# Local attention blocks: turned probabilities placed by DMAs, and half of the rotated keys' sum on VectorE

## What is computed

```
def attn_layer(x, Wqkv, qs, ksc, Wo):
    q, k, v = jnp.split(x @ Wqkv, 3, -1)         # then split into heads
    q = l2norm(q) * qs
    k = l2norm(k) * ksc
    q = q * cos * scale + rotate_half(q) * sin * scale
    k = k * cos * inv + rotate_half(k) * sin * inv
    out = local_attention(q, k, v)
    return out @ Wo
# local_attention: queries of window w against keys of windows w-1 and w
    sim = jnp.einsum('bhwie,bhwje->bhwij', bq, bk2) * QK_SCALE
    attn = jax.nn.softmax(jnp.where(mask, -max, sim), -1)
    out = jnp.einsum('bhwij,bhwje->bhwie', attn, bv2)
for i in range(6):
    x = attn_layer(shift_tokens(x), ...) + x
    x = ffn_layer(shift_tokens(x), ...) + x
```

## Time and profile before

| | us |
|---|---|
| median of 3 runs | 3162.67 |
| lowest, highest run | 3152.88, 3163.48 |
| the profiled execution, own time | 3146.83 |
| its span | 3144.8 |
| local blocks in it | 861 to 2760 |
| PE busy in the span | 2774.6 (88%) |
| DVE busy | 2442.2 (78%) |
| ACT busy | 2104.3 (67%) |
| POOL busy | 1351.6 (43%) |

### The profile page before, as it was taken

One profiled execution on the slowest core, in us unless ns is written; L12 is line 12 of the kernel. 1 busy time (PEld: TensorE's weight loads), 2 busy tenths in 40 slices (PEclk: granted clock), 3 DMA queues, 4 the chain that ended last, 5 costly groups with the idle time before them and its releaser, 6 DMA issues. The chain is left out here.

```text
span 3144.8 us, 72108 instructions
## 1 busy us (share of the span) xinstructions
PE 2774.6 (88%) x27244; PEld 1692.0 (54%) x27244; DVE 2442.2 (78%) x3071; ACT 2104.3 (67%) x3079; POOL 1351.6 (43%) x1209
## 2 busy tenths in 40 slices
PE   5799999997678989888889898989999999789997
PEld 3122222223546565656566666656665656478885
DVE  3899999992379797979798888888888979455554
ACT  2488888885158787878788787878787878311111
POOL 1000000000078685867586758676766767200000
PEclk7799999998589999999999999999999999889998
DMA  3011111100010001000100010001000000000001
GB/s 131 27 29 28 28 29 29 29 24 8 8 57 9 6 9 43 7 8 9 42 9 6 17 34 9 8 15 36 8 7 14 15 7 9 12 18 0 0 0 34
DMA packets 56465, 64.35 MB, mean 20 GB/s; under 512 B 24742, under 2 KB 38964, under 8 KB 55348
## 3 DMA queue, kind: packets, MB, share of 16 engines
q1 hardware_dynamic: 55380, 60.58, 7.0%
q10 hardware_dynamic: 864, 0.79, 0.1%
HBM read 36.69 MB, written 7.34 MB: 14 GB/s over the span
## 5 line engine op out<-in xcount | busy, mean ns | idle before, releaser
L886 DVE TENSOR_REDUCE a_minus_max<-a_ps_max 128x1 f32<-128x1024 f32 x512 | 596.8, 1218 | 57.6 <-PE a_ps_max L811 52.3
L794 ACT ACTIVATE a_expT<-a_ps_scoresT 128x512 f32<-128x512 f32 (+1 forms) x683 | 528.8, 808 | 78.2 <-PE a_ps_scoresT L829 67.4
L1178 POOL TENSOR_TENSOR b_turned_q<-b_rot_q,b_turned_q 128x1024 f32<-128x1024 f32 x96 | 226.8, 2362 | 270.2 <-DVE b_turned_q L1549 257.3
L844 PE MATMUL a_ps_out<-a_expT,v_aug 128*32 128x256 f32 x4096 | 327.9, 392 | 5.4 <-ACT a_outT L781 4.8
L1620 DVE STREAM_TRANSPOSE b_probsT<-b_probs 32x512 f32<-32x512 f32 x384 | 269.4, 702 | 11.9 <-POOL b_probs L1219 0.3
L765 POOL CAST a_max_hi<-a_minus_max 128x16 bf16<-128x16 f32 x32 | 6.3, 198 | 631.1 <-DVE a_minus_max L886 631.1
L1287 ACT ACTIVATE b_kT<-b_psD 64x512 f32<-64x512 f32 x384 | 226.1, 589 | 58.6 <-PE b_psD L1374 53.5
L829 PE MATMUL a_ps_scoresT<-a_q_op,a_k_op 26*128 26x512 bf16 x1024 | 247.2, 385 | 13.1 <-ACT a_expT L794 4.4
L1225 POOL TENSOR_TENSOR b_turned_k<-b_rot_k,b_turned_k 128x512 f32<-128x512 f32 x192 | 243.9, 1270 | 0.2 <-DVE b_turned_k L1549 0.2
L1185 POOL TENSOR_TENSOR b_rot_q<-b_turned_q,b_inv_norm 128x1024 f32<-128x1024 f32 x96 | 182.8, 1904 | 137.7 <-issue 137.7
L1219 POOL TENSOR_TENSOR b_probs<-b_probs,b_inv_sum 128x512 f32<-128x512 f32 x192 | 197.3, 1049 | 99.1 <-DVE b_inv_sum L1593 99.1
(11 more groups left out here) (295 smaller groups left out, 6019.4 us busy)
## 6 DMA issues: line engine op xcount, KB each, us to landing
b_v_edge<-b_v SPq DMA_DIRECT2D x96, 128.0 KB
b_w_qkv<-L_ffn_Wqkv SPq DMA_DIRECT2D x6, 1536.0 KB
a_q_op<-terms_q SPq DMA_DIRECT2D x128, 48.0 KB
a_k_op<-terms_k SPq DMA_DIRECT2D x128, 48.0 KB
joined<-a_outT SPq DMA_DIRECT2D x256, 16.0 KB
b_w_o<-L_ffn_Wo SPq DMA_DIRECT2D x6, 512.0 KB
a_q_op<-a_max_rows SPq DMA_DIRECT2D x128, 4.0 KB
b_w<-L_ffn_W SPq DMA_DIRECT2D x6, 341.0 KB
```

The costliest lines, as they stand in the source:

```text
L794: act.activation(expT[:, to:to + 512 * size], ps_scoresT[:, at:at + 512 * size], ACT.Exp, scale=SCALE_A).then_inc(exp_ready, 1)
L844: last_mm = pe.matmul(ps_out[lo:lo + 32, 256 * part:256 * part + 256], v_aug[:, b * T8 + kt, head, :], expT[:, at:at + 256], start=(kt == ...
L886: dve.tensor_reduce(minus_max[p % 2][:, side, 0, qt:qt + 1], ps_max[u % 2][:], AX.X, ALU.max, negate=True).then_inc(max_taken, 1)
L1178: pool.tensor_tensor(turned[:], rot[:], turned[:], ALU.add).then_inc(added, 1)
```

## The change

- Own windows: the four transposes of 32 partitions become one transpose of all 128 partitions into a new tile `packed_own`. Four DMAs on SP place its four parts in `probsT`.
- Windows before: the copies on ACT and POOL go. Four DMAs on SP place the parts of `packed`, one in `edgeT`, three in `probsT`.
- `probsT` is laid out by query window first, `[P, 4, 16, 32]`, so that each part is 2 KB in a row on each of 32 partitions. PE reads a head's four windows in four pieces.
- Keys' sum: of the two halves of eight heads, the first is added by DVE behind its sine part, the second by POOL as before. POOL scales both.
- The next layer's Wqkv comes as six DMAs of 256 KB, one behind each step 2 to 7 of the first batch, on SP's queue.
- The tile `ones` and its memset go, and counts of semaphores follow. PE waits for all eight DMAs ahead of the output product.

```diff
@@ sync
+                if 1 in lags:
+                    sp.wait_ge(packed_ready, T)
+                    if 2 in lags:
+                        sp.wait_ge(out_half, 2 * (T - 1))
+                    sp.dma_start(edgeT[P - W:P], packed[0:W]).then_inc(back_placed, 16)
+                    for j in range(1, P // W):
+                        sp.dma_start(probsT[W * j - W:W * j, j], packed[W * j:W * j + W]).then_inc(back_placed, 16)
+                    sp.wait_ge(packed_own_ready, T)
+                    for j in range(P // W):
+                        sp.dma_start(probsT[W * j:W * j + W, j], packed_own[W * j:W * j + W]).then_inc(own_placed, 16)
+                if b == 0 and not isinstance(s, int) and not (isinstance(l, int) and l == LAST):
+                    load_qkv_part(l + 1, (l + 1) % 2, s - 2)
...
-                    load_qkv(l + 1, (l + 1) % 2)
@@ gpsimd
-                    pool.wait_ge(out_half, 2 * (T - 2))
-                    pool.wait_ge(packed_ready, T - 1)
...
-                    for j in (2, 3):
-                        rows = slice(W * j, W * j + W)
-                        pool.tensor_tensor(probsT[W * j - W:W * j, :, rows], packed[rows], ones[rows]..., ALU.mult)
...
-                        pool.tensor_tensor(turned_k[:, heads], rot_k[:, heads], turned_k[:, heads], ALU.add).then_inc(sum_k_ready, 1)
-                        pool.wait_ge(sum_k_ready, 2 * T + half + 1)
+                        if half == 0:
+                            pool.wait_ge(low_sum_k_ready, T + 1)
+                        else:
+                            pool.tensor_tensor(turned_k[:, heads], rot_k[:, heads], turned_k[:, heads], ALU.add).then_inc(high_sum_k_ready, 1)
+                            pool.wait_ge(high_sum_k_ready, T + 1)
@@ scalar
-                    act.activation(edgeT[P - W:P], packed[0:W], ACT.Copy).then_inc(low_back_ready, 1)
-                    act.activation(probsT[0:W, :, W:2 * W], packed[W:2 * W], ACT.Copy).then_inc(low_back_ready, 1)
@@ tensor
-                    pe.wait_ge(probsT_ready, 4 * (T - 1))
-                    pe.wait_ge(low_back_ready, 2 * (T - 1))
-                    pe.wait_ge(high_back_ready, 2 * (T - 1))
+                    pe.wait_ge(own_placed, 64 * (T - 1))
+                    pe.wait_ge(back_placed, 64 * (T - 1))
@@ vector
                     rotary_sin(psK, turned_k, parts_k_ready, 2)
+                    dve.wait_ge(parts_k_ready, 2 * T + 2)
+                    dve.tensor_tensor(turned_k[:, 0:8], rot_k[:, 0:8], turned_k[:, 0:8], ALU.add).then_inc(low_sum_k_ready, 1)
...
                     dve.transpose(packed[:], probs[:, :, 0, :]).then_inc(packed_ready, 1)
...
-                    for j in range(P // W):
-                        rows = slice(W * j, W * j + W)
-                        dve.transpose(probsT[rows, :, rows], probs[rows, :, 1, :]).then_inc(probsT_ready, 1)
-                        if j == 0 and ahead:
-                            scale(ahead[0], ahead[1], 0)
+                    dve.transpose(packed_own[:], probs[:, :, 1, :]).then_inc(packed_own_ready, 1)
+                    if ahead:
+                        scale(ahead[0], ahead[1], 0)
```

More of the change, by code:

```diff
@@ L946, in local_blocks @@
         packed = sb("packed", [P, HEADS_B, W])
-        probsT = sb("probsT", [P, HEADS_B, P])
+        packed_own = sb("packed_own", [P, HEADS_B, W])
+        probsT = sb("probsT", [P, P // W, HEADS_B, W])
         edgeT = sb("edgeT", [P, HEADS_B, W])
-        ones = sb("ones", [P, HEADS_B])
         outT = sb("outT", [P, PAIRS, P])
@@ L991, in local_blocks @@
         sum_q_ready = sem("sum_q_ready")
-        sum_k_ready = sem("sum_k_ready")
+        low_sum_k_ready = sem("low_sum_k_ready")
+        high_sum_k_ready = sem("high_sum_k_ready")
         unit_q_ready = sem("unit_q_ready")
@@ L1007, in local_blocks @@
         packed_ready = sem("packed_ready")
-        probsT_ready = sem("probsT_ready")
-        low_back_ready = sem("low_back_ready")
-        high_back_ready = sem("high_back_ready")
+        packed_own_ready = sem("packed_own_ready")
+        back_placed = sem("back_placed")
+        own_placed = sem("own_placed")
         out_half = sem("out_half")
@@ L1084, in load_qkv, with load_qkv_part @@
                 sp.dma_start(w_qkv[:, ds(at, 3 * INNER)], wts["Wqkv"][ds(l, 1)].rearrange("o p n -> p (o n)")).then_inc(w_qkv_in, 16)
+            def load_qkv_part(l, slot, part):
+                at = slot * 3 * INNER + part * 512
+                sp.dma_start(w_qkv[:, ds(at, 512)], wts["Wqkv"][ds(l, 1), :, ds(part * 512, 512)].rearrange("o p n -> p (o n)")).then_inc(w_qkv_in, 16)
             def load_o(l):
@@ L1109, in step @@
             def step(l, b, s, par, lags, ahead=None):
+                T = l * TILES + b * T8 + s
                 if 0 in lags:
-                    T = l * TILES + b * T8 + s
                     sp.wait_ge(v_held, 2 * T + 2)
                     sp.dma_start(v_edge[par][P - W:P, :], v[1 - par][P - W:P, :]).then_inc(v_edge_in, 16)
+                if 1 in lags:
[10 more added lines that the diff above has]
+                    load_qkv_part(l + 1, (l + 1) % 2, s - 2)
             def middle(l, b):
@@ L1139, in _ @@
             load_mlp(0)
+            sp.wait_ge(zeroed, 9)
             stream(sp, step, middle)
@@ L1148, in _ @@
             pool.memset(edgeT[:], 0.0).then_inc(zeroed, 1)
-            pool.memset(ones[:], 1.0).then_inc(zeroed, 1)
             for i in range(2):
                 pool.memset(v_edge[i][:], 0.0).then_inc(zeroed, 1)
-            pool.wait_ge(zeroed, 8)
+            pool.wait_ge(zeroed, 7)
             for b in range(BATCHES):
                 pool.memset(y[64:P, column(b * T8):column(b * T8) + 1], 0.0).then_inc(zeroed, 1)
-            pool.wait_ge(zeroed, 10)
+            pool.wait_ge(zeroed, 9)
             def tokens_of(t, par):
@@ L1194, in step @@
                         pool.wait_ge(rope_ready, 4 * (l + 2) if after_tables else 4 * (l + 1))
[L1195 to L1198, removed]
-                    for j in (2, 3):
-                        rows = slice(W * j, W * j + W)
-                        pool.tensor_tensor(probsT[W * j - W:W * j, :, rows], packed[rows], ones[rows].unsqueeze(2).to_broadcast([W, HEADS_B, W]),
-                                           ALU.mult).then_inc(high_back_ready, 1)
-                        pool.wait_ge(high_back_ready, 2 * (T - 2) + j - 1)
                 if 0 in lags:
@@ L1239, in _ @@
         def _(act):
-            act.wait_ge(zeroed, 10)
+            act.wait_ge(zeroed, 9)
             def norm_start(l, b, n):
@@ L1267, in step @@
                         act.activation(qT[:, 4 * half:4 * half + 4, :].rearrange("p a b -> p (a b)"), psD[half][:], ACT.Copy).then_inc(qT_held, 1)
-                if 2 in lags:
-                    act.wait_ge(packed_ready, T - 1)
-                    act.wait_ge(out_half, 2 * (T - 2))
-                    act.activation(edgeT[P - W:P], packed[0:W], ACT.Copy).then_inc(low_back_ready, 1)
-                    act.activation(probsT[0:W, :, W:2 * W], packed[W:2 * W], ACT.Copy).then_inc(low_back_ready, 1)
                 if 0 in lags:
@@ L1337, in _ @@
         def _(pe):
-            pe.wait_ge(zeroed, 10)
+            pe.wait_ge(zeroed, 9)
             def mean(l, b, n, ended):
@@ L1363, in step @@
                 if isinstance(s, int) and s == 0 and b == 0 and 0 in lags:
-                    pe.wait_ge(w_qkv_in, 16 * (l + 1))
+                    pe.wait_ge(w_qkv_in, 16 + 16 * 6 * l)
                 w_at = l % 2 * 3 * INNER
@@ L1434, in step @@
                                 at = P * (pair % 4)
-                                pe.matmul(psD[half][rows, at:at + P], v[par][:, DH * head:DH * head + DH], probsT[:, head, :],
+                                pe.matmul(psD[half][rows, at:at + P].rearrange("p (j w) -> p j w", w=W), v[par][:, DH * head:DH * head + DH], probsT[:, :, head, :],
                                           start=(pair % 4 == 0), stop=False, skip_group_check=True)
@@ L1514, in _ @@
         def _(dve):
-            dve.wait_ge(zeroed, 10)
+            dve.wait_ge(zeroed, 9)
             def centre(l, b, n):
@@ L1572, in step @@
                     if 2 in lags:
-                        dve.wait_ge(probsT_ready, 4 * (T - 1))
+                        dve.wait_ge(packed_own_ready, T - 1)
                     rows = probs[:].rearrange("p h c k -> p h (c k)")
@@ L1610, in step @@
                     if 2 in lags:
-                        dve.wait_ge(low_back_ready, 2 * (T - 1))
-                        dve.wait_ge(high_back_ready, 2 * (T - 1))
-                        dve.wait_ge(out_half, 2 * (T - 1))
+                        dve.wait_ge(back_placed, 64 * (T - 1))
                     dve.transpose(packed[:], probs[:, :, 0, :]).then_inc(packed_ready, 1)
@@ L1617, in step @@
                     dve.wait_ge(probs_ready, 2 * T)
-                    for j in range(P // W):
-                        rows = slice(W * j, W * j + W)
```

(8 more changed lines are left out.)

## The result

The changed kernel takes 3173.71 us (median of 8 runs, 3167.06 to 3179.28), the kernel before 3150.64 (8 runs, 3144.27 to 3167.26, the three shown in front among them). The ratio is 1.0061, 95% interval 1.0036 to 1.0086: slower by 0.6%, where 1% faster was forecast. The time lies within the stated range, on the other side of no change. The profiled spans are 3167.0 and 3144.8 us.

What follows compares the result with a forecast made beforehand. PE's 1.66 us wait for POOL's keys in 82 steps was taken as the bound; steps of 15.45 instead of 15.91 us gave -38+5+2.4, about -30 us, so 3133 us, range 3108 to 3190.

Steps and rivals of the forecast that it cites:

- the floor: Output product to output product: 15.33 us however early POOL is, with ACT's square of K and key copies late next.
- The held sum: DVE's half sum, behind the sine part, waits for POOL's second product at X+8.20 (X: output product's start), done at X+8.89.
- the first rival: DVE's sum is not held: packed tile ready at X+8.6, the floor decides, 3117 us; chance 0.20.
- POOL's keys: POOL's sums and scalings of keys end about X+12.3 instead of X+12.9 (X: output product's start); PE's 1.66 us wait goes.
- The row of eight DMAs: SP, packed tile to output product: eight issues in 4.35 us, landing 1.35; step 15.45 us instead of 15.91, saving 38.
- break-even, 0.607 us: Time per DMA issue on SP from which the step passes 15.91 us and the change is slower.
- third rival: It comes to nothing: issues of 0.58 to 0.63 us or later landing, 3154 to 3185 us; 0.20 together with rival 4.
- the second one's mechanism: SP's issues between packed tile and output product are the bound: 0.66 us each, step 16.35, total 3206 us; chance 0.18.
- Ahead of the feed-forward parts: DVE's held sum makes the norm's chain start 0.45 us later, 11 times: 5 us lost.
- At the end: After the last block nothing covers the DMAs: PE's four transposes ended at 2706.99, now 2709.3; 2.4 us lost.
- SP's loads: Weights' load of 1.5 MB as six of 256 KB behind the placements: costed at nothing.
- The level: Median of the runs, 3162.67, taken as 16 us above the profiled execution, so 3117 became 3133.

Runs made afterwards that it cites:

- a: The changed kernel with DVE's half sum of the keys moved behind the packed transpose for the previous blocks: 3119.25 us, ratio 0.9902 to the kernel before.
- e: Kernel a with the half sum placed last, behind the scaled centred values, in the 11 steps ahead of a feed-forward part: 3095.76 us, ratio 0.9840 to before.
- f: The changed kernel with five placements instead of eight, three needed parts left out, so for timing only: 3101.35 us, ratio 0.9856 to before.

## Why the prediction was wrong, point by point

- **What bounded the kernel, and the floor.** Right. Kernels a, e and f run at the 15.33 us that were read from the step behind a feed-forward part.
- **The held sum.** Right in mechanism and size: 1.52 to 1.57 us in 95 of 96 steps, its end always 0.54 to 0.55 us behind POOL's products (0.7 forecast); 0.65 to 0.69 where POOL was idle (kernel a, 12 steps). POOL's products kept their 1.05 us. So the first rival falls. The Trainium skill, SBUF — State Buffer, section "Who interferes with whom", by which such a sum contends with POOL's reads of SBUF, is borne out here: 1.53 us beside POOL against 0.65 to 0.69.
- **POOL's keys.** End at X+12.30 (12.3). That PE's 1.66 us of waiting for them would be gone was wrong, 1.06 us stay, but ScalarE's first copies cover them.
- **The row of eight DMAs: the step that failed.** Start at X+9.51 (9.65 forecast), issues 4.94 us long (4.35 taken), landing and start 1.60 (1.40 taken): 16.05 instead of 15.40. In the 82 steps counted on, 0.6 us are about 50 us, nearly the whole way from the forecast's -30 us to the 22 measured between the spans. The pitch is 0.634 us. The two rows for it were right in front, 0.51 alone and 0.66 in a row, and I took the one with the same shape; what decides is that issues stand in a row. The first of a row takes 0.51 here too, each further one 0.59, and 0.044 lie between two. The prediction's own break-even, 0.607 us, stood between its two rows, so the sum had no sign yet. The outcome is its third rival, with the second one's mechanism.
- **Ahead of the feed-forward parts**, 5 us forecast, 3.1 measured, and that it came near is luck. In the step from 1334.28 the projection's sum starts at X+8.68, as in the kernel before, since X itself is late for the DMAs and POOL's products are early by it. The six stretches of each kernel in which the granted clock stays at 2.4 GHz take 39.94 to 40.10 us, 39.86 to 40.08 before, 0.1 us in all; the other 3.0 lie in the five in which the clock fell. **At the end**, 2.4 forecast, 3.0 measured.
- **SP's loads and fetches.** The six loads cost nothing that shows: the steps that have one have a median of 16.05 us, like the others. What no term held is the long steps, about 8 us more, most of them with a fetch packet beside the last placements. The prediction's path had no slack at its end.
- **The level.** The three runs shown of before lay high: 3150.64 is the median of eight, so the 16 us between profiled execution and median were too many. It doesn't bear on the sign.

The sum with the measured terms: 83 x 0.115 + 8.3 + 3.1 + 3.0 = 24 us, against 22 between the spans.

## What to carry to other kernels

Take the price of a DMA issue from a row of issues back to back, and when the break-even lies between two measured prices, forecast no change. Where a queue of DMAs replaces copies on engines, ask first what stands ahead of the instruction that starts it: here one operation of 0.7 us, moved behind that instruction, turned +0.6% into -1.0%. A second move made it -1.6%, of which about 6 us are shown to be its own. Leave some slack behind the last landing: the changed kernel, whose product waits for it, had 22 long steps; kernel a, whose product comes 0.82 us behind it, had 6.

## What the runs showed of the hardware

- An SBUF-to-SBUF DMA of 64 KB from 32 partitions: 0.51 us to issue as the first of a row (as long as the 128 KB of the edge values take alone), then one every 0.634 us; from the end of the last issue to the product that needs it 1.43 us with the DMAs alone (end of the blocks), 1.60 in the usual step, 1.81 with a ninth.

```profile
2727.15 2.49 SPq L1132 DMA_DIRECT2D b_probsT<-b_packed_own  x4
2731.07 1.98 PE L1438 MATMUL b_psD<-b_probsT,b_v 128*64 128x128 f32 x16 [8.65 <-DMA b_probsT<-b_packed_own]
```

- One instruction-fetch packet of 16 KB takes 0.9 to 1.4 us on one DMA engine (changed kernel, local blocks); where one falls beside the last placements, the last completion comes about a microsecond late (X+16.88 instead of X+15.84 in the two steps shown).
- PE ran at 1.2 GHz for parts of the first feed-forward products in 10 of 11 stretches when it had stood for 2.26 us (a), and in 4 of 11 when it had stood for 1.68 (e); with the same stand the clock fell in some stretches and not in others.
